# Constants on another queue, the sixth sweep streamed, a third pair of score banks, and a row of maxima by transposes, in a four-layer graph kernel

## The reference

```python
x = layernorm(x + inv_deg * (adj @ x + beta * x) @ K + bias)        # L0, inv_deg from row sums of adj
x = layernorm(x + relu(h3 + x))                                     # L1: h1, h2, h3 = gcn three times, 20 wide
x = layernorm(x + (adj * d^-1/2 * d^-1/2) @ (x @ W + b))            # L2
x = layernorm(x + adj @ x + gamma * softmax((x W_l)(x W_r)^T) @ x @ W_h @ W_g)   # L3
```

## Time and profile before

| | |
|---|---|
| median of 3 runs | 1466.33 us (1464.1 to 1467.71) |
| the profiled execution's own time | 1466.62 us |
| its span | 1464.8 us |
| PE busy | 94% of the span |
| sweep 0 | 0 to 268 us |
| sweeps 1 to 3 | 268 to 632 us |
| sweep 4 | 632 to 824 us |
| sweep 5 | 824 to 1016 us |
| attention, and the last layer norm within it | 1016 to 1464.8 us |

### The profile page before, as it was taken

How to read it: one execution, slowest core, us unless ns; L and a number is a source line. 1 busy time by engine, 2 the same in 40 slices (tenths; PEclk the granted TensorE clock), 3 DMA queues, 4 the chain that set the end, 5 groups by cost and what they waited for, 6 DMA issues and landing times.

```text
span 1464.8 us, 17014 instructions
## 1 busy us (share of the span) xinstructions
PE 1380.5 (94%) x5831; PEld 789.8 (54%) x5831; DVE 900.9 (61%) x1223; ACT 694.5 (47%) x875; POOL 235.7 (16%) x136
## 2 busy tenths in 40 slices
PE   6999999988898899999999999999799999999995
PEld 2555555312122222257777777777567667767753
DVE  3676777300000022488888977776888888888875
ACT  1101011101010111176777866665687878788776
POOL 0111111000000000000101000002033334333343
PEclk9999999999999999999999999999999999999998
DMA  9876677799999999998989889883000000000001
GB/s 345 321 274 230 249 279 266 294 409 407 407 408 408 408 395 397 395 328 312 317 313 324 296 278 327 317 314 129 0 1 1 0 1 1 1 1 1 1 1 58
DMA packets 101151, 337.30 MB, mean 230 GB/s; under 512 B 11354, under 2 KB 12890, under 8 KB 101082
## 3 DMA queue, kind: packets, MB, share of 16 engines
q1 hardware_dynamic: 101082, 336.40, 61.5%
HBM read 334.26 MB, written 2.10 MB: 230 GB/s over the span
## 4 chain that ended last, share of the span: by engine, by line
PE 65%; DMA 13%; DVE 11%; ACT 5%; issue 3%; SPq 2%; POOL 0%; DVEq 0%; ACTq 0%
DMA raw<-in_adj_s 13%; PE acc L1076 11%; PE acc L1112 9%; PE acc L1173 6%; PE acc L1168 6%; PE acc L1169 6%; PE acc L1096 4%; PE acc L1196 4%; DVE peak L861 4%; PE acc L1261 3%; DVE ring L885 3%; ACT ring L615 2%; ACT ring L603 2%; DVE t_lo L794 2%; PE e L989 1%
## 5 line engine op out<-in xcount | busy, mean ns | idle before, releaser
L794 DVE TENSOR_TENSOR t_lo<-raw,t_hi 128x1024 fp32r<-128x1024 f32 x224 | 275.3, 1251 | 61.1 <-ACT t_hi L554 56.8
L554 ACT ACTIVATE t_hi<-raw 128x1024 fp32r<-128x1024 f32 x224 | 234.1, 1058 | 72.7 <-PE acc L1173 71.2
L1168 PE MATMUL acc<-t_hi,st_hi 128*128 128x512 f32 x448 | 201.7, 450 | 2.9 <-DVE st_lo L699 2.9
L475 POOL TENSOR_TENSOR ring_lo<-ring,p_hi 128x1024 fp32r<-128x1024 f32 x64 | 155.5, 2429 | 271.3 <-ACT p_hi L609 271.3
L1076 PE MATMUL acc<-raw,x 128*128 128x512 f32 x384 | 173.3, 606 | 14.6 <-DMA raw<-in_adj_s 14.6
L1112 PE MATMUL acc<-raw,h_a 128*20 128x512 f32 x736 | 162.5, 598 | 22.8 <-DMA raw<-in_adj_s 22.6
L1169 PE MATMUL acc<-t_hi,st_lo 128*128 128x512 f32 x448 | 175.3, 391 | 0.0
L725 DVE TENSOR_TENSOR xs<-e,bias 128x512 f32<-128x512 f32 x8 | 5.5, 690 | 267.0 <-PE e L992 267.0
L499 ACT ACTIVATE at<-acc 128x512 f32<-128x512 f32 x48 | 28.7, 597 | 289.4 <-PE acc L1112 180.9
L885 DVE TENSOR_TENSOR ring<-ring,e 128x1024 f32<-128x1024 f32 x128 | 154.2, 1210 | 0.1
L603 ACT ACTIVATE ring<-ring 128x1024 f32<-128x1024 f32 x128 | 134.7, 1054 | 36.9 <-DVE ring L885 36.8
(11 more groups left out here) (182 smaller groups left out, 2099.1 us busy)
## 6 DMA issues: line engine op xcount, KB each, us to landing
raw<-in_adj_s SPq DMA_DIRECT2D x584, 512.0 KB, 7.3
resident<-in_adj_s SPq DMA_DIRECT2D x16, 512.0 KB, 7.4
raw<-in_adj_s SPq DMA_DIRECT2D x24, 256.0 KB, 7.7
kept_t<-in_adj_s SPq DMA_DIRECT2D x8, 512.0 KB, 5.9
x<-in_x SPq DMA_DIRECT2D x4, 512.0 KB, 8.1
kept_s<-in_adj_s SPq DMA_DIRECT2D x8, 256.0 KB, 6.1
kept_v<-in_adj_s SPq DMA_DIRECT2D x8, 256.0 KB, 6.4
kept_l<-in_adj_s SPq DMA_DIRECT2D x8, 256.0 KB, 9.0
```

The costliest lines, as they stand in the source:

```text
L475: nc.gpsimd.tensor_tensor(ring_lo[:, n % RING, :], slot(n), p_hi[:, m % 2, :].bitcast(F32), ALU.subtract).then_inc(pl_done, 1)
L554: nc.scalar.activation(t_hi[:, (par * NS + g) % HL, :], raw[:, k, :], ACT.Copy).then_inc(hi_done, 1)
L794: nc.vector.tensor_tensor(t_lo[:, k, :], raw[:, slot_no(s, c, g), :], t_hi[:, k, :].bitcast(F32), ALU.subtract).then_inc(lo_done, 1)
L1168: mm(a[:, :], block_of(st_hi, b), hi[:, m], start=(b == 0), stop=False)
```

## The change

What it does, part by part:

1. **Constants.** The 18 constant loads go from SP's list to the start of ACT's list, behind a wait for the last part of `x0` and ahead of ACT's four copies of `x0`. SP goes from tile 7 to the kept loads and tile 8.
2. **Sixth sweep.** Sweep 5 streams all 16 tiles of a chunk, all split, through all 8 slots; `resident` isn't read there. Two more `st_hi`/`st_lo` pairs are made in its first chunk.
3. **Start of the attention.** In ticks 0 to 14 the scores rotate over three pairs of banks (`rs01`, `e23`, and the two accumulators as `acc01`), then over two as before. `k_lo` is made by POOL, between its `add_one` instructions. The value parts (`values_hi`, `values_lo`) are made five ticks later.
4. **Row of maxima.** The four diagonal blocks are dropped; PE transposes, four times, one column of `m4` read 128 times over.
5. **Order of `out_proj`.** The four one-column products come first, with a semaphore of their own.
6. **Last layer norm.** In three parts: blocks 0 to 15 and 16 to 23 on POOL, two or three at a time between its `weights_lo`, during the sixth and the last block of queries; the Sqrt of these parts in ticks 94 and 124. The last 8 blocks at the end, 5 on DVE and 3 on ACT. The finish of query block 6 comes seven ticks later.

The diff, cut to its core:

```diff
@@ slots and waits of the stream
+        def wide_tiles(s):
+            return NG if s == S5 else NS
...
+            return g % RAW_4 if s == S4 else g % RAW if s == S5 else tile_no(s, c, g) % RAW
...
+            elif s == S5 and first(c) and g == RAW_4:
+                sp.wait_ge(pe_tile, T_WIDE)
+            elif s == S5 and not (first(c) and g < RAW_4):
+                sp.wait_ge(lo_done, wide_no(s, c, g) - (RAW - 1))
@@ last layer norm
-        LN_PARTS = ((0, NB - CB), (NB - CB, NB))
-        ACT_LN = {NT + 9: (0, 4), NT + 11: (4, 8), NT + 13: (8, 12), NT + 15: (12, 16)}
-        DVE_LN = {NT + 9: (16, 19), NT + 11: (19, 22), NT + 13: (22, 25), NT + 15: (25, 28)}
+        LN_PARTS = ((0, 16), (16, 24), (24, NB))
+        LN_SCALES = (NT - 34, NT - 4)
+        POOL_LN = {NT - 53: (0, 3), NT - 51: (3, 6), NT - 49: (6, 9), NT - 47: (9, 12), NT - 45: (12, 14), NT - 43: (14, 16),
+                   NT - 15: (16, 18), NT - 13: (18, 20), NT - 11: (20, 22), NT - 9: (22, 24)}
+        LN_LAST = (NB - 2 * CB, NB - 3, NB)
@@ score banks
+        def score_bank(t):
+            return (rs01, e23, acc01)[t % 3] if t < KP - 1 else (e23, rs01)[t % 2]
+        def same_bank_earlier(t):
+            if t < 3:
+                return None
+            return t - 3 if t <= KP else t - 2
@@ sync, then gpsimd
-                        if g == RAW:
-                            for dst, src in consts:
-                                sp.dma_start(dst[:, :], src).then_inc(const_in, 16)
...
+            for c in range(1, NC):
+                keys_lo(c)
+                if c >= NC // 2:
+                    add_one(c - NC // 2)
             for n in range(NT):
                 if n % KP in SPLIT:
                     weights_lo(n)
+                if n in POOL_LN:
+                    normalise_first(*POOL_LN[n])
@@ scalar
+            act.wait_ge(x_in[XP - 1], 16)
+            for dst, src in consts:
+                nc.scalar.dma_start(dst[:, :], src).then_inc(const_in, 16)
...
+                if t in LN_SCALES:
+                    last_deviation(LN_SCALES.index(t))
@@ vector, in tick
-            ticks(tick, keys_lo)
+            ticks(tick)
...
-                for b in range(CB):
-                    n = nc.vector.tensor_scalar(block_of(diag, b), ident[:, :], m4[:, b:b + 1], None, ALU.mult)
-                n.then_inc(diag_done, 1)
@@ tensor
+                    if s == S5:
+                        continue
...
+                if same_bank_earlier(t) is not None:
+                    pe.wait_ge(s_copied, same_bank_earlier(t) + 1)
+                    pe.wait_ge(s_maxed, same_bank_earlier(t) + 1)
...
             def peak_row(i):
-                pe.wait_ge(diag_done, i + 1)
-                mm(free_banks[i % 2][:, :], ones_f[:, :], diag[:, :], start=True, stop=True).then_inc(row_mm, 1)
+                pe.wait_ge(m4_done, i + 1)
+                for b in range(CB):
+                    n = mm(block_of(free_banks[i % 2], b), m4[:, b:b + 1].broadcast_to([P, P]), ident[:, :],
+                           is_transpose=True, start=True, stop=True)
+                n.then_inc(row_mm, 1)
```

More of the change, by code:

```diff
@@ L36 @@
 RAW = 8
-RAW_W = 7
+RAW_4 = 7
 HL = 4
@@ L386, in step @@
             def step(s, c, par):
-                for g in range(NT_N if s in FLAT else NS):
+                for g in range(NT_N if s in FLAT else wide_tiles(s)):
                     if s == 0 and first(c):
@@ L406, in _ @@
             chunks(sp, step)
-            for n, (a, b, by_act) in enumerate(RESULT):
-                if by_act:
-                    sp.wait_ge(fin_xa, sum(r[2] for r in RESULT[:n]) + 1)
-                else:
-                    sp.wait_ge(fin_x, sum(not r[2] for r in RESULT[:n]) + 1)
+            for a, b, by, count in RESULT:
+                sp.wait_ge({"fin_x": fin_x, "fin_xa": fin_xa, "fin_xp": fin_xp}[by], count)
                 sp.dma_start(out[:, a * D:b * D], v[:, a * D:b * D]).then_inc(out_done, 16)
@@ L459, in _, with keys_lo, add_one, normalise_first @@
             keep_old_x(5, NC - 1)
-            def add_one():
-                pool.wait_ge(pe_acc, NC * NSWEEP)
-                pool.wait_ge(S["xb"], done("xb", 5, NC - 1))
-                for c in range(NC // 2):
-                    part = cols(x, c, 2 * CW)
-                    nc.gpsimd.tensor_tensor(blocks(part, NC), blocks(part, NC),
-                                            ones_f[:, :].unsqueeze(1).broadcast_to([P, NC, D]),
-                                            ALU.add).then_inc(v1_done, 1)
+            def keys_lo(c):
+                pool.wait_ge(k_hi_done, c + 1)
+                nc.gpsimd.tensor_tensor(cols(k_lo, c - 1), cols(v, c), cols(k_hi, c - 1).bitcast(F32),
+                                        ALU.subtract).then_inc(k_lo_done, 1)
+            def add_one(j):
+                part = cols(x, j, 2 * CW)
+                nc.gpsimd.tensor_tensor(blocks(part, NC), blocks(part, NC),
+                                        ones_f[:, :].unsqueeze(1).broadcast_to([P, NC, D]),
+                                        ALU.add).then_inc(v1_done, 1)
+            def normalise_first(a, b):
+                pool.wait_ge(fin_nmr, 1 if b <= LN_PARTS[0][1] else 2)
+                for n in range(a, b):
+                    i = nc.gpsimd.tensor_scalar(block_of(v, n), block_of(xf, n), rstd_a[:, n:n + 1],
+                                                nmr_a[:, n:n + 1], ALU.mult, ALU.add)
+                if b in [r[1] for r in RESULT]:
+                    i.then_inc(fin_xp, 1)
             def weights_lo(n):
@@ L545, in step @@
                 ps, pc = before(s, c)
-                for g in range(NS):
+                for g in range(wide_tiles(s)):
                     if s not in FLAT:
@@ L1160, in wide_sweep @@
                 pe.wait_ge(S["at"], done("at", s, c) - 2)
-                for g in range(NS):
-                    hi, lo = t_hi[:, (par * NS + g) % HL, :], t_lo[:, (par * NS + g) % HL, :]
+                for g in range(wide_tiles(s)):
+                    k = (par * wide_tiles(s) + g) % HL
+                    hi, lo = t_hi[:, k, :], t_lo[:, k, :]
                     if first(c):
-                        pe.wait_ge(st_lo_done, NS * (s - len(FLAT)) + g + 1)
+                        pe.wait_ge(st_lo_done, NS * (s - S4) + g + 1)
                     pe.wait_ge(hi_done, wide_no(s, c, g) + 1)
```

128 lines of the change are left out of this document (63 added, 65 removed).

## The result

The median of the changed kernel is 1441.12 us (1440.57 to 1445.9, four executions), of the kernel before 1466.58 (1464.1 to 1467.71): a ratio of 0.9836, 95% interval 0.9812 to 0.986, 25.5 us less. The execution that was profiled is the one of 1445.9; the other three have spans of 1439.0 to 1439.6 and not 1444.3. The first experiment is about that difference.

A forecast was written before the change was run, and what follows sets the result against it. PE work was taken as the bound (65% of the span, 13% the `adj` stream; the stream limits sweeps 1 to 3). Terms summed to -30.2 us from 1466.6, so 1436.4, forecast 1436; 8-in-10 range 1427 to 1447.

The forecast's parts named there:

- Constants, -6.2 forecast: Start: moving constants off SP's queue lands tile 8 at 26.5, clock kept, chunk 0 ending 41.1 against 47.3: -6.2 us.
- rival D: Start: constants cost the stream as before, tile 8 lands at 29 with the clock lost: 1441 us, chance 0.11.
- The cover of `bx`: Start: ACT's later `x0` copies stay hidden, POOL's `bx` done by 35 and PE wanting it near 38.
- Sweep 5, -5.3: Sixth sweep: streaming all tiles saves 0.69 us a chunk, 0.2 taken off for the first chunk: -5.3 us.
- B: Sweep 5: the stream bounds it at 342 GB/s, a chunk taking 24.5 us: +8, 1450 us, chance 0.08.
- C: Sweep 5: the stream stays at 311 GB/s, a chunk taking 27.0 us: +27, slower at 1469, chance 0.03.
- Attention's start, -7.1: First attention ticks: third bank lifts the latency limit, scores 15 end 6.0 us earlier, first maxima row 1.1: -7.1.
- A: Attention's start and tail: POOL slow, `k_lo` and `add_one` 1.5 times their rows, norm block 1 us: 1445, chance 0.11.
- Square roots, +4.7: Ticks 94 and 124: Sqrt table loads on ACT delay the copy before the fold, 2.5 and 2.2 us: +4.7.
- E: Attention: better than laid out, third bank at PE's pace (-3.7 more), table loads hidden (-4.7): 1428, chance 0.09.
- F: Ticks 94 and 124: a table load costs more when ACT is full, 2.5 us more each: 1441, chance 0.03.
- Tail, -12.3: Last fold to last `bt`: POOL does the norm, PE holds 3.10 for two ticks, 35.9 against 49.0, 0.8 given back.

The follow-up runs named there:

- The first experiment: The changed kernel run again twice with nothing altered, to read its profile in other executions: medians 1440.59 and 1441.97 us.
- tiles_before_kept: Changed kernel with the five kept loads of chunk 0 issued behind tiles 8 to 11 instead of ahead of them: 1440.39 us.
- best_two: Changed kernel with `k_lo` on VectorE, tiles before kept loads in chunks 0 and 1, table-free 1/sqrt, weighted products before last transposes: 1435.54 us, ratio 0.9791.
- after: First profile of the changed kernel itself, against the kernel before, taken in its execution of 1445.9 us; median 1441.12 us.
- no_mid_sqrt: Changed kernel with a plain copy in place of the square root for 24 of the 32 last layer norm blocks: 1436.2 us.
- diagonal_row: Changed kernel with the row of maxima made as before, from four diagonal blocks on VectorE and one product with ones: 1449.35 us.
- again: The changed kernel run once more with nothing altered, on its own: 1440.59 us.

## Why the prediction was right, and where its terms were off

The sign and the range held; the point was 5 us too low. By its own steps:

*Constants, -6.2 forecast: -2.7 in the first profile, -3.9 at most.* This is the term that was most off. "I take 26.5" for the landing of tile 8 stood between two worked-out ends; PE started on it at 27.9, near rival D's 29. And "a gap of 4 us is shorter than the one in which the clock fell, so I let it stand" had no row behind it: at 5.17 the clock fell (0.51), and it fell at 3.42 too (0.80 in its window). D had roughly the size of this term, -1.7 where it was -2.7, but not the cause. D and the term put the fall from 407 to 250 GB/s down to the constants' small packets. In the changed kernel the same constants go out from 17 to 27 us, beside the stream, and the rate is 374 and 391 GB/s. What differs is SP's list. Before, it held nothing but constants from 7.21 to 19.82, and tile 8 came behind them. Most of the wait that is left comes from the 2.1 MB of kept blocks, as `tiles_before_kept` shows. That the stream ran out of issued loads where it fell to 250 is the likeliest reading; no run took it apart. The Trainium skill (DMA: Bandwidth & Descriptors, "Issuing engines are not separate DMA queues") has a second issuing engine save the issue time only. The rows agree with it: 12.6 us of issuing left SP's list, and the gain, 2.6 to 4.5 us, stays below that.

*The cover of `bx`.* It was named as hidden, with the product done by 35 and wanted near 38. It was done at 40.4 and wanted at 42.0, 1.6 us of cover. `best_two` bears out the sentence behind it, that each microsecond would be PE's if the cover went: PE waits 6.56 there.

*Sweep 5, -5.3: -6.5.* The mechanism held, the resident blocks cost more than their own 3.43 us: 0.91 a chunk against 0.69. The rows place most of the 0.22 more at the resident blocks. In `after`, 13 tiles with nothing between them take 17.68 us of PE (starts 904.17 and 921.85), 1.36 each, and a chunk has 22.67 - 16 x 1.36 = 0.91 beside them. With that, the kernel before is left with 23.58 - 14 x 1.36 - 0.91 = 3.63 for its four resident blocks, 0.20 more than the 3.43 of their own pace: 0.05 at each block, where PE passes from one kind of product to the other and back. What happens there no row shows. B and C are wrong: 362 GB/s at a share of 0.96, and nobody waits for it. The 342 of the earlier trace rows was the demand, not what the stream could give.

*Attention's start, -7.1: -5.6* (4.95 to the first fold, 0.62 in the first period). The third bank did what was said. GpSimd was a little slower than laid out (`k_lo` 1.29 for 1.25), and the `v_lo` beside it on VectorE took 1.91 instead of 0.41, after which PE waited 0.85. A was the right place, at under a third of its price (1.5 of 5.1).

*Middle, -4.2: -4.55*, the sum over periods 2 to 7 in `no_mid_sqrt`. `diagonal_row` shows that nearly all of it is this part's: 0.48 in period 2 and 0.77 to 0.79 in periods 3, 4, 5 and 7.

*Square roots, +4.7: +4.8* (2.55 and 2.27). E's and F's views of them are both wrong, and so is 5.3 us a place, which the Trainium skill gives for two table loads (ScalarE: Activation LUTs, "Table sets: the hidden batching unit"): two loads and the root are 2.8 us in the rows, and the cost is a little less. Its advice, to batch by set, holds all the same: without the loads these 4.8 us are gone. The loads sit two ticks ahead of a fold, where the copy of a score is on the path, and they make the gap of 2.5 us at the fold behind which the clock fell in five of the ten profiles that have them.

*Tail, -12.3: -12.8 without a fall of the clock, -11.25 with it.* GpSimd's norm block took 0.47 on average where 0.35 was taken. The pace of 3.10 was reached. Part of the gain is the kernel before's own fall of the clock in its tail, which the working didn't name.

*End, +0.2: +0.9.* `out_proj` first gave 0.3 where 0.5 was taken, the blocks on DVE cost 0.3 as said, and the stretch from the first issue of the last output to the end of the span is 3.27 us in `again`, with two transfers, against 2.35 before, with one: 0.9 where 0.4 was taken.

The measured terms sum to -2.7 - 6.5 - 5.6 - 4.55 + 4.8 - 12.8 + 0.9 = -26.5, and with one fall of the clock, 1.2 to 1.6, about -25: the medians differ by 25.5. What the sum lacked was a term for the clock behind the folds. Besides, the constants (3.5), the attention's start (1.5) and the end (0.7) came out worse than forecast, by 5.7 together, and 2 us of that are hidden because sweep 5, the middle and the tail came out better than forecast: there the misses cancel by luck. The range holds for all that. Its upper end is lower than its own reason, though: A and D together add 13 to 1436, which is 1449 and not 1447.

## What to carry to other kernels

When a load is late, count the bytes queued ahead of it and ask of each whether its consumer needs it sooner. Moving one load from in front of another moves the wait to whatever was landing next, as tile 8, the kept blocks, tile 12 and the last constant took turns here. A small wait on the busiest engine can have a second price, in its clock, so a table load or a reduction should not end at a place where that engine has nothing else to do.
